# Moving two steps of layer 1 in ScalarE's hand-written order of a graph-attention kernel

## The chip, the cores and the metric

The kernel runs on one core of a Trainium2 chip. The metric is the device time of one execution in microseconds (us); less is better. The kernel before was timed three times: 405.50, 405.58 and 405.77 us, so its median is 405.58 us.

Of the core's engines, TensorE (PE) does the matrix products and writes to PSUM, VectorE (DVE) and GpSimd (POOL) do elementwise work and reductions, ScalarE (ACT) does activations, copies and scalings, and SyncE (SP) only starts transfers here. Each engine works off its own list of instructions in order and waits at semaphores for the others.

## The reference

Sixteen graphs of 512 nodes with 128 features each pass through four layers; every layer adds its input and normalizes each node:

```python
x = _layernorm(x + _L0_gnn_ref(x, adj, ...))   # attention, softmax over a row
x = _layernorm(x + _L1_gnn_ref(x, adj, ...))   # attention, softmax over a column, ELU
x = _layernorm(x + _L2_gnn_ref(x, adj, ...))   # attention, softmax over a row, ELU
x = _layernorm(x + _L3_gnn_ref(x, ...))        # sums over relations, no softmax
```

The change lies in layer 1:

```python
h = x @ W;  s1 = h @ a1;  s2 = h @ a2
e = leaky_relu(s1[:, :, None] + s2[:, None, :], 0.2)
att = softmax(where(adj > 0, e, -9e15), axis=1)     # over the column
h_prime = att @ h
return elu(h_prime)
```

A column without any edge gets equal weights in this softmax (all its entries are -9e15). The kernel calls it an empty column and fills it.

## The kernel before, in words

**Items and slots.** One graph in one layer is an item; items are numbered n = layer * 16 + graph, so layer 1 is items 16 to 31. Each engine runs the function `attention_slot(at, n)` for slot after slot; `at(k)` is item n + k. So in slot n an engine does the late steps of items n-3 to n and the early steps of items n+1 to n+4, in an order that is written out by hand and that is its own for each engine. A slot of layer 1 takes about 7.2 us.

**The way of a layer-1 item k.**
- Slot k-4 and k-3: PE transposes x (L482), ACT copies it (`take_xT`, L720), PE multiplies by the weights (L503), ACT copies the result to `hx` (`take_h`, L725). DVE takes the maximum of a score per partition (`own_max`, L1008), PE spreads it, DVE reduces it to `smax` (`take_max`, L1013).
- Slot k-2: from the scores and `smax`, ACT makes `col_tmp[ABOVE]` by a Relu (`above_max`, L756) and from it `col_tmp[HINGE]` by an Exp (`column_hinge`, L761, the hinge). POOL adds the mark of the empty columns to it and gets `col_tmp[WEIGHT]` (`column_weight`, L313). POOL also makes `col_tmp[BELOW]` (`below_max`, L306).
- Slot k-1: PE spreads BELOW over `rows_ps` (`spread_rows`, L551). ACT makes two exponentials of it, one in `q_rows` (L770) and one in place (L771); together they are `take_rows`. POOL masks the first quarter of the edges (`mask_rows`, L298). DVE makes the other three quarters in `edges` (L1024, three instructions; each needs WEIGHT and the rows) and then the four blocks of the matrix `PT` in `weights` (L1041 for block 0, L1047 for blocks 1 to 3), with the sums of the columns beside them. From these come the reciprocals `col_tmp[RZ]` (`column_sums` L1069, `column_factors` L1073). ACT adds the mark of empty columns to block 0 of `PT` (`fill_empty`, L777; the other blocks get it from DVE by a maximum).
- Slot k: POOL scales h by RZ (`scale_h`, L281), and PE multiplies (`attend`, L566), once `PT` is whole, filled and h scaled.
- Slot k+1: ACT begins the ELU (`elu`, L789 Relu, L799 Exp), POOL adds to it (`elu_low`, L337), DVE finishes the sum (`add_elu`, L1122), takes the moments (`finish` L1128, `aggregate` L1135).
- Slot k+2: POOL makes the reciprocal deviation (`find_rstd`, L319 and L322), ACT scales to the new x (`take_scaled`, L806, four instructions).

**Order on POOL** in a slot of layer 1: `below_max(n+2)`, `mask_rows(n+1)`, `elu_low(n-1)`, `find_rstd(n-2)`, `column_weight(n+2)`, `scale_h(n+1)`. After `scale_h` comes the next slot's `below_max`. **Order on DVE:** `own_max(n+3)`, the four blocks of `PT` of item n+1, `take_max(n+3)`, `column_sums`, `column_factors`, `add_elu(n-1)`, and from slot 17 on the three edge instructions of item n+2 among the moments of item n-1; in slots 15 to 17 the edges of item n+1 stand at the head of the slot. **Order on PE:** transposes, `spread_rows(n+1)`, `project(n+3)`, `attend(n)`. **Order on ACT** before, for layer 1: `take_rows(n+1)`, `elu(n-1)`, `take_h(n+3)`, `take_xT(n+4)`, `above_max(n+2)`, `take_scaled(n-2)`, `fill_empty(n+1)`, `column_hinge(n+2)`.

At the start of layer 1 ACT's slot 15 ends with `flag(15)` (L839, a 2 us pass over the mask), and at the end slots 30 and 31 have `node_factors` of layer 2 (L735 to L751) in them.

Of the kernel before, what the change touches and what calls it, by code (L numbers as in the profile page):

```python
# [54 lines left out]
def build(nc, x, adj, adj_rows, w_in, w_out, a_in, b2, ab2, w3, b3, out):  # L55
    ctx = ExitStack()
    with ctx:
# [8 lines left out]
        def sem(name):  # L66
            if name not in sems:
                sems[name] = ctx.enter_context(nc.semaphore(name))
            return sems[name]
# [628 lines left out]
        def _(act):  # L698
# [34 lines left out]
            def node_factors(it):  # L733
                act.wait_ge(sem("smax"), it.done)
                act.activation(shifts[:, it.b, :], shift_k[:, 0:3], ACT.Copy, scale=smax[:, it.b:it.b + 1])\  # L735
                    .then_inc(sem("shifts"), 1)
                act.wait_ge(sem("shifts"), halves(it))
                if it.l > 0 or it.g >= 2:

                    act.wait_ge(sem("PT"), (it.done - 2) * C)  # L740
                    act.wait_ge(sem("h_scaled"), it.done - 2)
                raw = factors_raw[:, it.b, :, :]
                act.activation(raw[:, 0, :], hx[:, it.r, :, S1], ACT.Relu, scale=1 - SLOPE,
                               bias=shifts[:, it.b, 0:1])
                act.activation(raw[:, 1, :], hx[:, it.r, :, S2], ACT.Exp, scale=1 - SLOPE,
                               bias=shifts[:, it.b, 1:2])
                act.activation(raw[:, 2, :], hx[:, it.r, :, S2], ACT.Exp, scale=SLOPE,
                               bias=shifts[:, it.b, 2:3]).then_inc(sem("factors_raw"), 1)
                act.wait_ge(sem("factors_raw"), halves(it))
                act.activation(factors[:, it.b, 0, :], raw[:, 0, :], ACT.Exp, scale=-1.0)  # L750
                act.activation(factors[:, it.b, 1:3, :], raw[:, 1:3, :], ACT.Identity, bias=floor_col[:, 0:1])\  # L751
                    .then_inc(sem("factors"), 1)

            def above_max(it):
                act.wait_ge(sem("smax"), it.done)
                act.activation(col_tmp[:, it.b, ABOVE, :], hx[:, it.r, :, S2], ACT.Relu, bias=smax[:, it.b:it.b + 1])\  # L756
                    .then_inc(sem("above"), 1)

            def column_hinge(it):
                act.wait_ge(sem("above"), it.of_layer)  # L760
                act.activation(col_tmp[:, it.b, HINGE, :], col_tmp[:, it.b, ABOVE, :], ACT.Exp, scale=SLOPE - 1)\  # L761
                    .then_inc(sem("hinge"), 1)

            def take_rows(it):
                act.wait_ge(sem("rows_ps"), it.done)
                if it.g >= 1:

                    act.wait_ge(sem("edge_lin"), (it.of_layer - 1) * EDGES)
                    act.wait_ge(sem("mask_rows"), (it.of_layer - 1) * WHOLE)
                act.activation(q_rows[:, :], rows_ps[:], ACT.Exp, scale=SLOPE).then_inc(sem("q_rows"), 1)  # L770
                act.activation(rows_ps[:], rows_ps[:], ACT.Exp, scale=1 - SLOPE).then_inc(sem("rows_taken"), 1)  # L771

            def fill_empty(it):

                act.wait_ge(sem("PT"), (it.done - 1) * C + WHOLE)
                for c in range(WHOLE):
                    last = act.activation(PT[:, it.b, c, :], PT[:, it.b, c, :], ACT.Identity,  # L777
                                          bias=empty_col[:, it.g, c:c + 1])
                last.then_inc(sem("filled"), 1)

            def elu(it):

                if it.l > 1 or it.g >= 1:
                    act.wait_ge(sem("elu_exp"), it.done - (G + 1))

                if it.l == 1:
                    act.wait_ge(sem("att"), it.done)
                    lin_ps = o_ps[it.b][:, :, 1:1 + D]
                    act.activation(elu_low_arg[:, :, :], lin_ps, ACT.Relu, scale=-1.0)\  # L789
                        .then_inc(sem("elu_low_arg"), 1)  # L790
                else:
                    act.wait_ge(sem("y_lin"), it.of_layer)
                    act.activation(elu_low_arg[:, :, :], lin[:, it.b, :, :], ACT.Relu, scale=-1.0)\
                        .then_inc(sem("elu_low_arg"), 1)

                if it.done > G + 1:
                    act.wait_ge(sem("y_sum"), it.done - 1)
                act.wait_ge(sem("elu_low_arg"), it.done - G)
                act.activation(elu_exp[:, :, :], elu_low_arg[:, :, :], ACT.Exp, scale=-1.0)\  # L799
                    .then_inc(sem("elu_exp"), 1)  # L800

            def take_scaled(it):

                act.wait_ge(sem("rstd"), it.done)
                for c in range(C):
                    last = act.activation(X[:, it.g, c, :], y[:, it.t, c, :], ACT.Copy, scale=rstd[:, it.t, c:c + 1])  # L806
                last.then_inc(sem("x_new"), 1)

            def take_norm(it):
                act.wait_ge(sem("offset"), it.of_layer)  # L810
                for c in range(C):
                    last = act.activation(X[:, it.g, c, :], y[:, it.t, c, :], ACT.Identity,  # L812
                                          bias=offset[:, it.t, c:c + 1], scale=rstd[:, it.t, c:c + 1])
                last.then_inc(sem("x_new"), 1)
# [28 lines left out]
            def take_bias2(n):  # L843

                for k, part in enumerate((bias2_hi, bias2_mid, bias2_low)):
                    if n == BIAS_SLOT + 5 + k:
                        act.wait_ge(sem("bias2"), 5)
                        row = slice(32 * k, 32 * k + 1)
                        act.copy(bias2_parts[row, 0:130], part[row, :])
                        act.copy(bias2_parts[row, 130:260], part[row, :])  # L850
                        act.activation(bias2_parts[row, 260:260 + D], part[row, 0:D], ACT.Copy, scale=float(N))\
                            .then_inc(sem("bias2_parts"), 1)

            def take_next(at):
                if at(3):
                    take_h(at(3))
                if at(4):
                    take_xT(at(4))
                if at(4) and at(4).done == 1:
                    take_folded_weights()  # L860

            def attention_slot(at, n):
                if at(1) and at(1).l == 1:
                    take_rows(at(1))
                if at(-1) and at(-1).l == 1:
                    elu(at(-1))
                if at(2) and at(2).l in (0, 2):
                    node_factors(at(2))
                if at(-1) and at(-1).l == 2:
                    elu(at(-1))  # L870
                past_first_layer = any(at(k) and at(k).l >= 1 for k in (1, -2))
                if past_first_layer:
                    take_next(at)
                take_bias2(n)
                if at(2) and at(2).l == 1:
                    above_max(at(2))
                if at(-3) and at(-3).l == 0:
                    take_scaled(at(-3))
                if at(-3) and at(-3).l == 2:
                    take_norm(at(-3))  # L880
                if at(-2) and at(-2).l == 1:
                    take_scaled(at(-2))
                if at(1) and at(1).l == 1:
                    fill_empty(at(1))
                if not past_first_layer:
                    take_next(at)
                take_centred(n)
                if at(2) and at(2).l == 1:
                    column_hinge(at(2))
                if n == -1:  # L890
                    act.wait_ge(sem("b2_ps"), 1)
                    act.copy(b2_a[:, :], o_ps[1][:, 0, 0:2]).then_inc(sem("b2_a"), 1)
                if at(0) and at(0).l == 0:
                    flag(at(0))
# [85 lines left out]
            def redo_norm(g, k):  # L980
# [5 lines left out]
                last.then_inc(sem("re_x"), 1)  # L986

            pipeline(attention_slot, FIRST, LAST_ATTENTION, G * LAYERS)
            pipeline(last_layers(attention_slot, relation_slot), LAST_ATTENTION, ALL_STEPS, G * (LAYERS + 1))
            act.wait_ge(sem("out"), 16 * G)  # L990
            with act.If(not_binary(act)):
# [399 lines left out]
```

## Time and profile before

| | |
|---|---|
| median of three runs | 405.58 us |
| the profiled execution | 405.65 us |
| its span, first to last instruction | 403.5 us |
| busy: DVE, PE, ACT, POOL | 87%, 88%, 77%, 76% of the span |
| layer 1 in the span | about 112 to 230 us |
| ACT's steps `take_rows`, `fill_empty`, hinge | 0.99, 0.61 and 0.10 us, start to next start |

The profile shows one execution. Each instruction has a start in us from the beginning of the span, a duration, an engine, a line of the kernel, and, in brackets, how long its engine had been idle before it and which instruction of which engine ended that. Durations of neighbours on one engine overlap a little, so that the distance from start to start is the better price of an instruction in a row. "L313" is line 313 of the kernel. The busy shares are means over all layers; what a step is worth is read from its own stage.

### The profile page before, as it was taken

The page shows a single profiled execution, that of the slowest core. Times are in us where ns is not written, and L with a number is a line of the kernel's source. Part 1 is how long each engine was busy: PE and PEld are TensorE (multiplying, and loading weights), DVE is VectorE, ACT ScalarE, POOL GpSimd, SP SyncE. Part 2 cuts the span into 40 slices and gives each one's busy share as a digit, 9 for nine tenths or more (in the row PEclk, how much of TensorE's full clock was granted, in tenths as well). Part 3 has the DMA queues.
Part 4 walks back from the last instruction along what each step waited for, and adds up shares of the span by engine and source line. Part 5 has one row for each costly group of instructions (what it writes and reads, how often), then busy time and mean ns, then how long its engine had stood idle before and what let it go on. Part 6 is the DMA issues. An engine that isn't in the chain of part 4 may idle for free. (4 is left out here: it accounts for less than half of the span.)

```text
span 403.5 us, 9212 instructions
## 1 busy us (share of the span) xinstructions
PE 354.2 (88%) x2784; PEld 315.7 (78%) x2791; DVE 350.3 (87%) x1350; ACT 310.3 (77%) x845; POOL 306.8 (76%) x399
## 2 busy tenths in 40 slices
PE   7798999999977878788788889999999879799990
PEld 7697999999977778778687889999998776466660
DVE  0558899999999989999999988999999997799975
ACT  2757999999886676776877867688988846888851
POOL 5356888787779778687675776888888885899992
PEclk9999999999999999999999999999999989999997
DMA  6999983000000000000000000000000000012223
GB/s 172 202 246 246 249 167 54 2 1 2 2 1 2 1 2 0 2 2 0 1 2 2 3 0 2 0 3 2 0 4 2 0 2 0 0 72 86 80 79 109
DMA packets 8755, 18.19 MB, mean 45 GB/s; under 512 B 1280, under 2 KB 2560, under 8 KB 8704
## 3 DMA queue, kind: packets, MB, share of 16 engines
q0 software_dynamic: 2304, 8.39, 10.9%
q1 hardware_dynamic: 5280, 8.72, 6.2%
q10 hardware_dynamic: 1120, 0.46, 0.5%
q8 instruction: 24, 0.39, 0.4%
q14 instruction: 27, 0.22, 0.2%
HBM read 21.76 MB, written 4.19 MB: 64 GB/s over the span
## 5 line engine op out<-in xcount | busy, mean ns | idle before, releaser
L566 PE MATMUL o_ps<-h_scaled,PT 128*128 128x129 f32 (+1 forms) x1536 | 182.3, 277 | 9.9 <-POOL h_scaled L281 7.3
L566 PEld LDWEIGHTS o_ps<-h_scaled,PT 128*128 128x128 f32 x1536 | 176.7, 193 | 12.7 <-issue 10.6
L1052 DVE SCALAR_TENSOR_TENSOR PT<-rows_ps,factors,MT 128x512 f32<-128x512 f32 x128 | 89.2, 739 | 0.0
L806 ACT ACTIVATE X<-y,rstd 128x128 f32<-128x128 f32 x184 | 58.4, 389 | 24.7 <-POOL rstd L322 24.7
L322 POOL TENSOR_TENSOR rstd<-var_eps,neg_half 128x4 f32<-128x4 f32 x64 | 70.1, 1095 | 5.0
L503 PE MATMUL h_ps<-wx,xT 128*128 128x130 f32 x384 | 53.5, 283 | 13.8 <-DVE smax L1013 12.2
L503 PEld LDWEIGHTS h_ps<-wx,xT 128*128 128x128 f32 x384 | 48.3, 193 | 19.6 <-issue 19.3
L1128 DVE BATCH_NORM_STATS2 stats<-y 128x6 f32<-128x128 f32 x256 | 55.6, 280 | 5.8 <-DVE y L1122 0.9
L257 POOL TENSOR_TENSOR mean_term<-h_mean,empty_row 128x512 f32<-128x512 f32 x32 | 38.2, 1194 | 9.9 <-DVE residual L1108 5.2
L337 POOL TENSOR_TENSOR elu_exp<-elu_exp,X 128x512 f32<-128x512 f32 x32 | 40.8, 1276 | 5.1 <-ACT elu_exp L799 4.8
L281 POOL TENSOR_TENSOR h_scaled<-hx,factors 128x516 f32<-128x516 f32 x32 | 33.6, 1052 | 12.7 <-PE o_ps L566 8.2
L1024 DVE SCALAR_TENSOR_TENSOR edge<-rows_ps,col_tmp,q_rows 128x512 f32<-128x512 f32 x48 | 34.8, 736 | 4.0 <-ACT rows_ps L771 3.7
L725 ACT COPY hx<-h_ps 128x520 f32<-128x520 f32 x48 | 27.7, 577 | 10.5 <-PE h_ps L507 10.1
L1047 DVE SCALAR_TENSOR_TENSOR PT<-MT,empty_col,edge 128x512 f32<-128x512 bf16 x48 | 34.6, 765 | 0.0
L319 POOL TENSOR_TENSOR var_eps<-mean_var,eps_tile 128x4 f32<-128x4 f32 x64 | 18.3, 286 | 18.8 <-DVE mean_var L1135 18.6
L839 ACT ACTIVATE square_out<-MT,minus_half 128x2048 bf16<-128x2048 bf16 x16 | 32.0, 1998 | 0.0
L482 PE MATMUL xT_ps<-ident,X 128*128 128x128 f32 x192 | 30.0, 280 | 0.9 <-ACT xT L720 0.9
L720 ACT ACTIVATE xT<-xT_ps 128x512 f32<-128x512 f32 x48 | 28.6, 596 | 0.0
L812 ACT ACTIVATE X<-y,offset,rstd 128x128 f32<-128x128 f32 x64 | 26.2, 488 | 1.4 <-POOL offset L331 1.4
L1135 DVE BATCH_NORM_AGGREGATE mean_var<-stats 128x2 f32<-128x6 f32 x256 | 23.9, 156 | 2.3
L1008 DVE TENSOR_REDUCE smax_own<-hx 128x1 f32<-128x4 f32 x48 | 7.0, 147 | 20.6 <-ACT hx L725 20.6
L482 PEld LDWEIGHTS xT_ps<-ident,X 128*128 128x128 f32 x192 | 23.0, 145 | 1.7 <-ACT xT L720 1.6
(123 smaller groups left out, 660.6 us busy)
## 6 DMA issues: line engine op xcount, KB each, us to landing
MT<-adj_by_j POOLq DMA_DIRECT2D x16, 512.0 KB, 14.8
X<-x SPq DMA_DIRECT2D x16, 256.0 KB, 8.1
out<-X SPq DMA_DIRECT2D x16, 256.0 KB, 2.0
w_rel<-w SPq DMA_DIRECT2D x1, 256.0 KB, 6.0
w_back<-w_by_output ACTq DMA_DIRECT2D x1, 192.0 KB, 3.5
wx<-w_by_input ACTq DMA_DIRECT2D x1, 192.0 KB, 4.0
bias<-b ACTq DMA_DIRECT2D x1, 64.0 KB, 3.0
bias_in<-b SPq DMA_DIRECT2D x1, 64.0 KB, 8.3
```

The costliest lines, as they stand in the source:

```text
L257: pool.tensor_tensor(mean_term[:, it.b, :, :], h_mean[:, it.m, :].unsqueeze(1).broadcast_to([P, C, D]), empty_row[:, it.g, :].unsqueeze(2) ...
L281: pool.tensor_tensor(h_scaled[:, it.b, :, first:1 + D], hx[:, it.r, :, first:1 + D], by.unsqueeze(2).broadcast_to([P, C, 1 + D - first]), ...
L322: pool.tensor_tensor(rstd[:, it.t, :], var_eps[:, it.t, :], neg_half[:], ALU.pow)\
L337: pool.tensor_tensor(elu_exp[:, :, :], elu_exp[:, :, :], X[:, it.g, :, :], ALU.add)\
L482: last = pe.transpose(xT_ps[:, c * P:(c + 1) * P], rows[:, c, :], ident[:])
L503: last = pe.matmul(h_chunk_ps(c, 130), xT[:, b, c * P:(c + 1) * P], wx[:, l, :], start=(l != 2), stop=(l != 2 or c == 1))
L566: last = pe.matmul(o_ps[it.b][:, ic, first:1 + D], PT[:, it.b, jc, ic * P:(ic + 1) * P], h_scaled[:, it.b, jc, first:1 + D], start=(jc == ...
L806: last = act.activation(X[:, it.g, c, :], y[:, it.t, c, :], ACT.Copy, scale=rstd[:, it.t, c:c + 1])
L1024: dve.scalar_tensor_tensor(out=edge[:, c, :], in0=rows_ps[:], scalar=col_tmp[:, it.b, WEIGHT, c:c + 1], in1=q_rows[:, :], op0=ALU.max, op1 ...
L1047: dve.scalar_tensor_tensor(out=PT[:, it.b, c, :], in0=m, scalar=empty_col[:, it.g, c:c + 1], in1=edge[:, c, :], op0=ALU.max, op1=ALU.min, ...
L1052: dve.scalar_tensor_tensor(out=PT[:, it.b, c, :], in0=rows_ps[:], scalar=factors[:, it.b, 1, c:c + 1], in1=m, op0=ALU.max, op1=ALU.mult, * ...
L1128: last = dve.bn_stats(stats[:, c, :], y[:, b, c, :])
```

## The change

On ScalarE, in the slots of layer 1, two steps are moved. `column_hinge(n+2)` goes from the end of the slot to just behind `above_max(n+2)`, from whose result it is made. `fill_empty` goes from behind `take_scaled` to the second place of the next slot, behind `take_rows` and ahead of `elu`; since the slot number has gone up by one, it is called with `at(0)` there instead of `at(1)`. ACT's order in a slot becomes `take_rows(n+1)`, `fill_empty(n)`, `elu(n-1)`, `take_h`, `take_xT`, `above_max(n+2)`, `column_hinge(n+2)`, `take_scaled(n-2)`. No instruction is added or removed, and no other engine's list changes.

```diff
@@ def attention_slot(at, n):   # ScalarE
                 if at(1) and at(1).l == 1:
                     take_rows(at(1))
+                if at(0) and at(0).l == 1:
+                    fill_empty(at(0))
                 if at(-1) and at(-1).l == 1:
                     elu(at(-1))
...
                 if at(2) and at(2).l == 1:
                     above_max(at(2))
+                    column_hinge(at(2))
...
                 if at(-2) and at(-2).l == 1:
                     take_scaled(at(-2))
-                if at(1) and at(1).l == 1:
-                    fill_empty(at(1))
                 if not past_first_layer:
                     take_next(at)
                 take_centred(n)
-                if at(2) and at(2).l == 1:
-                    column_hinge(at(2))
```

## Rows read from the trace of the kernel before

**Rows 1.** Who waited for whom, 142 to 223 us (total us, times, longest us)
```profile
POOL col_tmp L313 <- ACT col_tmp L761: 22.9, 12, 2.1
ACT X L806 <- POOL rstd L322: 18.1, 11, 2.0
...
DVE edge L1024 <- ACT rows_ps L771: 3.5, 10, 0.9
```
**Rows 2.** Timeline of POOL, 199.9 to 207.3 us (start us, duration us, instruction, idle before)
```profile
199.94 0.20 POOL L313 TENSOR_TENSOR col_tmp<-col_tmp,big_col 128x4 f32<-128x4 f32 x1 [2.10 <-ACT col_tmp L761]
200.09 1.04 POOL L281 TENSOR_TENSOR h_scaled<-hx,col_tmp 128x512 f32<-128x512 f32 x1
...
202.51 1.28 POOL L337 TENSOR_TENSOR elu_exp<-elu_exp,X 128x512 f32<-128x512 f32 x1
...
204.02 1.03 POOL L322 TENSOR_TENSOR rstd<-var_eps,neg_half 128x4 f32<-128x4 f32 x1
207.15 0.20 POOL L313 TENSOR_TENSOR col_tmp<-col_tmp,big_col 128x4 f32<-128x4 f32 x1 [2.10 <-ACT col_tmp L761]
```
**Rows 3.** Timeline of ACT, 203.8 to 209.3 us
```profile
203.79 0.30 ACT L756 ACTIVATE col_tmp<-hx,smax 128x4 f32<-128x4 f32 x1
205.09 1.28 ACT L806 ACTIVATE X<-y,rstd 128x128 f32<-128x128 f32 x4 [0.99 <-POOL rstd L322]
206.27 0.71 ACT L777 ACTIVATE PT<-PT,empty_col 128x512 f32<-128x512 f32 x1
206.88 0.19 ACT L761 ACTIVATE col_tmp<-col_tmp 128x4 f32<-128x4 f32 x1
206.98 0.57 ACT L770 ACTIVATE q_rows<-rows_ps 128x512 f32<-128x512 f32 x1
...
207.97 0.58 ACT L789 ACTIVATE elu_low_arg<-o_ps 128x512 f32<-128x512 f32 x1
208.64 0.63 ACT L799 ACTIVATE elu_exp<-elu_low_arg 128x512 f32<-128x512 f32 x1
```
**Rows 4.** Timeline of DVE: a passage without wait, then a steady slot
```profile
134.30 0.68 DVE L1122 SCALAR_TENSOR_TENSOR y<-o_ps,elu_exp 128x512 f32<-128x512 f32 x1
135.06 0.75 DVE L1024 SCALAR_TENSOR_TENSOR edge<-rows_ps,col_tmp,q_rows 128x512 f32<-128x512 f32 x1
...
200.86 0.75 DVE L1024 SCALAR_TENSOR_TENSOR edge<-rows_ps,col_tmp,q_rows 128x512 f32<-128x512 f32 x1 [0.27 <-ACT rows_ps L771]
...
204.61 0.74 DVE L1047 SCALAR_TENSOR_TENSOR PT<-MT,empty_col,edge 128x512 f32<-128x512 bf16 x1
...
207.02 0.18 DVE L1073 RECIPROCAL col_tmp<-col_tmp 128x4 f32<-128x4 f32 x1
207.11 0.68 DVE L1122 SCALAR_TENSOR_TENSOR y<-o_ps,elu_exp 128x512 f32<-128x512 f32 x1
```
**Rows 5.** Timeline of PE, 201.4 to 206.2 us
```profile
201.39 3.81 PE L566 MATMUL o_ps<-h_scaled,PT 128*128 128x128 f32 x32 [0.41 <-POOL h_scaled L281]
...
205.58 0.60 PE L551 MATMUL rows_ps<-ident,col_tmp 128*128 128x128 f32 x4
```
**Rows 6.** Timelines of POOL and DVE where small POOL work meets L1047
```profile
133.35 1.42 POOL L322 TENSOR_TENSOR rstd<-var_eps,neg_half 128x4 f32<-128x4 f32 x1
...
154.25 0.39 POOL L345 TENSOR_TENSOR bias<-b_a,ab_sb 128x2 f32<-128x2 f32 x1
...
154.52 0.74 DVE L1047 SCALAR_TENSOR_TENSOR PT<-MT,empty_col,edge 128x512 f32<-128x512 bf16 x1
...
168.69 0.62 POOL L351 TENSOR_TENSOR bias_rest<-bias,bias_hi 128x130 f32<-128x130 f32 x1
...
168.94 0.91 DVE L1047 SCALAR_TENSOR_TENSOR PT<-MT,empty_col,edge 128x512 f32<-128x512 bf16 x1
```
**Rows 7.** Timelines of ACT and DVE near the end of layer 1
```profile
224.94 0.57 ACT L725 COPY hx<-h_ps 128x520 f32<-128x520 f32 x1
...
225.54 0.16 DVE L1008 TENSOR_REDUCE smax_own<-hx 128x1 f32<-128x4 f32 x1
```

## The prediction

> **What bounds the kernel now.** I read the table of waits for the steady part of layer 1 first, then the timelines of POOL, ACT and DVE over one of its slots, then PE's, and last the two ends of the layer. The reader is to see a ring of two engines. In the waits [rows 1], POOL's `column_weight` waits 22.9 us for ACT's hinge, and ACT's `take_scaled` waits 18.1 us for POOL's rstd: each of the two idles for the other, which is the mark of a closed ring. DVE waits only 3.5 us in ten slots, always for `take_rows`. So DVE is nearly full, and the ring is what keeps it from being quite full.
>
> The ring can be added up from one slot. POOL goes from `column_weight` at 199.94 through `scale_h`, `below_max`, `mask_rows`, `elu_low`, `var_eps` to rstd, which starts at 204.02 and takes 1.03, without a gap: 5.11 us [rows 2]. ACT takes over at 205.09 (0.04 later) with `take_scaled`, 1.18 us from start to the next start; then the fill, 0.61; then the hinge, 0.19 [rows 3]; and POOL's next `column_weight` starts at 207.15, 0.08 behind the hinge's end [rows 2]. 5.11 + 0.04 + 1.18 + 0.61 + 0.19 + 0.08 = 7.21 us, which is the distance of the two `column_weight` rows. The hinge needs neither `take_scaled` nor the fill: its input, `above_max`, was done at 204.09, while ACT then idled 0.99 us [rows 3]. It merely stands behind them in ACT's list.
>
> DVE's own list is shorter. From the first edge instruction at 200.86 to the end of `add_elu` at 207.79 it runs for 6.93 us [rows 4]. Where nothing is waited for, the next edge instruction starts 0.08 behind the end of `add_elu` (134.98 to 135.06) [rows 4]. So DVE alone would take 7.01 us a slot, 0.20 less than the ring.
>
> **The change part by part.** Nothing is added or removed, so the sum is about order only.
>
> *The hinge moved up.* It will stand behind `above_max` and wait for its result. The nearest row for such a step is the ELU's Exp, which starts 0.09 behind the end of the Relu it needs (208.55 to 208.64) [rows 3]. So the hinge runs about 0.3 us after the start of `above_max`, at the place of today's 204.2, done at 204.4, all of it inside ACT's idle time before rstd (0.98 to 1.9 us in these slots) [rows 1, 3]. Cost nothing; if that cover were gone it would cost 0.3 us of ACT. `column_weight` then has its input before POOL gets to it, and POOL does it right behind rstd. The ring is opened. What is late next for `scale_h` is its other input, RZ from DVE: done at 207.20, where POOL now starts `scale_h` near 207.30 (207.15 plus the 0.15 from row to row) [rows 2, 4]. With 0.08 for the semaphore, it would start at 207.28: POOL's chain is from now on hung on DVE.
>
> *The fill moved back.* `take_rows` comes 0.61 + 0.10 us earlier behind `take_scaled`, at today's 206.27 instead of 206.98 [rows 3]. It also needs `rows_ps` from PE, whose four transposes end at 206.18 [rows 5], 0.09 before. Then follow the two exponentials, 0.99, the fill, 0.61, and the ELU at its old place: 206.27 + 0.99 + 0.61 = 207.87 against 207.97. So the ELU isn't delayed against rstd, though the fill stands in front of it. The fill ends at 206.27 + 0.99 + 0.71 = 207.97; PE's `attend` also needs h_scaled, which ends 1.04 after 207.28, at 208.32. The fill has 0.35 us in hand and costs nothing. Queued behind `take_rows`'s wait are now the fill and with it `attend`: PE gives `rows_ps` in its list before `attend`, so there is no circle.
>
> *What this does to a steady slot.* I lay out a slot with the first edge instruction at 0 and 7.01 us of DVE. RZ is done at 6.34; `scale_h` starts at 6.42, which is 0.59 before the next edge (before, 200.09 to 200.86: 0.77 before it) [rows 2, 4]. Rstd ends 4.96 later, at 4.37 of the next slot; `take_scaled` starts at 4.41; `take_rows` runs from 5.59 to 6.6 and a bit (0.48 plus 0.58). DVE wants it at 7.01: 0.35 us in hand. Other rings: from rstd over `take_scaled` 1.18, `take_rows` 0.99, the fill 0.61, the ELU 0.67 + 0.63, 0.08, and `elu_low` to the end of rstd, 202.51 to 205.05, 2.54, plus 0.04: 6.74 us. PE from `attend` to the end of `spread_rows`, 201.39 to 206.18, 4.79 [rows 5], then `take_rows` and fill 1.70 and 0.3 to the next `attend`: 6.8 us. All below 7.01, so DVE alone sets the pace.
>
> *The sum.* The ten waits of DVE come to 3.5 us [rows 1]; each leaves the 0.08 that is there anyway: 3.5 - 0.8 = 2.7 us. Two more slots of the twelve show no wait; I count them at nothing. The largest piece is the first, the 0.9 us [rows 1], where ACT has two `take_scaled` in a slot. The slots before it, 15 to 17, gain nothing: DVE is not kept waiting there.
>
> *The end of the layer.* In the fill's last place nothing changes: in slot 31 there is no `take_rows`, so the fill of item 31 has the same neighbours. But ACT's later part of a slot now lies later against DVE: the ELU starts 0.17 after the next edge instruction (4.41 + 1.18 + 0.99 + 0.61 = 7.19, less 7.01, about 0.18), where before it started 0.10 before it (207.97, edge at 208.07). That is 0.28 later. In most slots `hx` has room for it, but in slot 30, with layer 2's factors in ACT's list, `hx` is done at 225.51 and DVE's `own_max` takes it at 225.54 [rows 7]. DVE waits there some 0.25 us, and POOL's chain behind RZ hands it on to layer 2. Bounds for this piece: 0 (if ACT's lag is smaller) and 0.3. I take 0.25. 2.7 - 0.25 = 2.45 us. Behind layer 1 all engines hang on DVE and POOL, and no transfer is due, so I carry the gain to the end unchanged; an estimate, with 0.3 either way.
>
> *A new neighbour.* `column_weight` will run right behind rstd, 4.37 us after the edge, and DVE's first L1047 starts at 3.75 (204.61 less 200.86) and takes 0.74 [rows 4], so that the second starts at about 4.4. Before, it ran when DVE was past its L1047s. The nearest rows are a 128x2 operation of POOL in that very place, 154.25, with 0.39 instead of 0.20, and the L1047 beside it, unhurt at 0.74; and a larger one, 128x130 with two inputs, at 168.69, beside which L1047 took 0.91, 0.17 more [rows 6]. `column_weight` is 128x4, nearest to the first: I take 0 and keep 0.17 a slot. POOL has 2 us to spare there. Such an overlap is the case of a rule of the Trainium skill (SBUF — State Buffer, Who interferes with whom): a VectorE instruction with two SBUF inputs and a GpSimd instruction that reads SBUF exclude each other, and the one that starts first blocks the other. By that rule `column_weight` would wait for the first L1047 and might hold up the second; the row at 154.25 agrees for the first half of it and not for the second. If it held in full, with the 0.20 of `column_weight` lost at L1047 in each of twelve slots, the sum would be 2.4 us worse, 405.6.
>
> 405.65 - 2.45 = 403.2 us. The profiled execution, 405.65, is 0.07 above the median of the runs, 405.58, so I leave it at 403.2.
>
> **The rivals.**
> - *DVE is hurt by the new neighbour.* Each of the twelve steady slots loses 0.17 us at L1047: 2.0 of the 2.45 us are given back, 405.2 us. For it: the row of 0.91 [rows 6]. Against: it stands beside an operation of thirty times the size.
> - *Nothing gained.* The wait for `take_rows` would stay because `rows_ps` is late: PE's rows are only 0.09 us ahead of the new need [rows 3, 5]. If `spread_rows` came 0.55 later than I lay out, the 0.35 in hand and the 0.20 of gain would be gone: 405.6. Against: `spread_rows` hangs on `scale_h` by a fixed 4.79 + 0.26 us, which I have counted.
> - *Slower: POOL slides into DVE's L1047.* POOL's chain lies 0.18 us later against DVE. Rstd took 1.42 instead of 1.03 where it began inside an L1047 (133.35) [rows 6]. If var_eps and rstd both slid in and took 0.4 more each, the ring over fill and ELU would be 6.74 + 0.8 = 7.54 us, 0.33 above today's slot, 12 x 0.33 = 4.0: 409.6 us. The point from which it decides: the chain would have to start 0.7 us later against DVE (rstd begins at 3.34 and var_eps 0.3 ahead of it, the first L1047 at 3.75 [rows 4]). Against: a steady shift of 0.18 is what the sum gives. The same rule of the Trainium skill bears on it, and the 1.42 agrees with it.
> - *More than I say.* No loss at the layer's end, the two uncounted slots give their few hundredths, and layer 2 starts better: 402.6.
>
> **How the numbers follow.** Forecast 0.62 (402.9 to 403.7); more gain 0.09; neighbour 0.12; nothing 0.11; slower 0.06. A change within 0.2% (0.8 us) is about what a measurement of this kernel can't tell from none. Of the neighbour's share a third lies past 0.8 us, since it need not cost the full 0.17. Faster 0.75, same 0.18, slower 0.07. The range from 402.4 to 405.2 takes in the forecast, more gain and the neighbour, and leaves out nothing and slower, 0.17.
>
> **What would show it.** Right: POOL's L313 loses its 22.9 us of waits for L761, and L281 waits for DVE's L1073 instead, up to 2 us a slot; L1024's waits for L771 vanish; slots of 7.0 us; ACT still waits for rstd about 1.5 us. At the end of the layer L1008 waits 0.2 to 0.3 for L725. Wrong: L1047 of 0.9 beside L313; L319 of 0.6 or L322 of 1.4 in the steady slots; PE waiting for the fill; slots that stay at 7.2.

## The result, and the profile after

The changed kernel takes 401.75 us (median of 8 runs, 400.24 to 403.54); the kernel before took 405.50 us beside it (8 runs, 404.32 to 405.77). The ratio is 0.9903, with a 95% interval of 0.9885 to 0.9921: faster by 3.75 us. The forecast was 403.2 us in a range of 402.4 to 405.2, so the sign and the mechanism were right and the size was not: the gain was half as large again as forecast. The profiled execution took 401.82 us with a span of 399.7 us, against 405.65 and 403.5 before: 3.83 us by the one and 3.8 by the other.

First the waits of the steady part of layer 1 in the changed kernel, 139 to 221 us, as in [rows 1] (engine, line, waited for whom: total us, times, longest us; VectorE's line numbers are one lower than before, those of POOL, PE and of the ACT rows shown here are the same):

```profile
ACT X L806 <- POOL rstd L322: 13.3, 12, 1.5
POOL h_scaled L281 <- DVE col_tmp L1072: 11.5, 12, 1.8
...
PE o_ps L566 <- ACT PT L777: 0.5, 1, 0.5
DVE edge L1023 <- ACT rows_ps L771: 0.2, 1, 0.2
```

POOL's 22.9 us of waits for the hinge [rows 1] are gone, and POOL waits for VectorE's reciprocals instead. VectorE's 3.5 us have shrunk to 0.2. The ring of POOL and ACT is open; VectorE now sets the pace. PE's wait of 0.5 us for the fill comes once, at 142.91, near the start of the stretch, and so does VectorE's 0.2.

The timeline of VectorE in a steady slot, which answers to [rows 4], shows how full it is (start, duration, instruction):

```profile
183.05 0.68 DVE L1121 SCALAR_TENSOR_TENSOR y<-o_ps,elu_exp 128x512 f32<-128x512 f32 x1
183.65 0.74 DVE L1023 SCALAR_TENSOR_TENSOR edge<-rows_ps,col_tmp,q_rows 128x512 f32<-128x512 f32 x1
...
189.80 0.18 DVE L1072 RECIPROCAL col_tmp<-col_tmp 128x4 f32<-128x4 f32 x1
189.89 0.68 DVE L1121 SCALAR_TENSOR_TENSOR y<-o_ps,elu_exp 128x512 f32<-128x512 f32 x1
190.49 0.74 DVE L1023 SCALAR_TENSOR_TENSOR edge<-rows_ps,col_tmp,q_rows 128x512 f32<-128x512 f32 x1
```

From edge to edge are 6.84 us, not the 7.01 of the forecast. The edge instruction starts 0.60 us after `add_elu` started, which is 0.08 before the record of `add_elu` ends. The forecast had it 0.08 behind that end.

The chain that feeds VectorE, on ACT and POOL, as in [rows 2, 3]:

```profile
187.14 1.03 POOL L322 TENSOR_TENSOR rstd<-var_eps,neg_half 128x4 f32<-128x4 f32 x1
188.14 0.73 POOL L313 TENSOR_TENSOR col_tmp<-col_tmp,big_col 128x4 f32<-128x4 f32 x1
190.05 1.04 POOL L281 TENSOR_TENSOR h_scaled<-hx,col_tmp 128x512 f32<-128x512 f32 x1 [1.19 <-DVE col_tmp L1072]
```
```profile
188.20 1.28 ACT L806 ACTIVATE X<-y,rstd 128x128 f32<-128x128 f32 x4 [0.93 <-POOL rstd L322]
189.39 0.57 ACT L770 ACTIVATE q_rows<-rows_ps 128x512 f32<-128x512 f32 x1
189.86 0.58 ACT L771 ACTIVATE rows_ps<-rows_ps 128x512 f32<-128x512 f32 x1
```

`take_rows` ends at 190.44, and VectorE's edge instruction starts at 190.49. So the chain has no time in hand at all any more: it and VectorE's own list arrive together. And at the end of the layer, as in [rows 7] (VectorE, then ACT):

```profile
221.50 0.16 DVE L1007 TENSOR_REDUCE smax_own<-hx 128x1 f32<-128x4 f32 x1 [0.53 <-ACT hx L725]
```
```profile
220.90 0.57 ACT L725 COPY hx<-h_ps 128x520 f32<-128x520 f32 x1
```

### The profile page after: what moved, and what is told of

Its sections match the earlier page's. It is cut to its first block and busy times, and to the rows that moved or that the text cites. A ratio compares the mean times of both kernels' runs of the same rounds, so it can differ in the third digit from the quotient of the medians.

```text
span 399.7 us, 9212 instructions
## 1 busy us (share of the span) xinstructions
PE 354.1 (89%) x2784; PEld 315.8 (79%) x2791; DVE 349.2 (87%) x1350; ACT 311.5 (78%) x845; POOL 313.5 (78%) x399
## 5 line engine op out<-in xcount | busy, mean ns | idle before, releaser
L503 PEld LDWEIGHTS h_ps<-wx,xT 128*128 128x128 f32 x384 | 48.3, 193 | 17.1 <-issue 16.9
L1046 DVE SCALAR_TENSOR_TENSOR PT<-MT,empty_col,edge 128x512 f32<-128x512 bf16 x48 | 34.5, 763 | 0.0
L281 POOL TENSOR_TENSOR h_scaled<-hx,col_tmp 128x512 f32<-128x512 f32 x16 | 16.7, 1042 | 14.2 <-DVE col_tmp L1072 14.2
```

The source lines that it names most:

```text
L281: pool.tensor_tensor(h_scaled[:, it.b, :, first:1 + D], hx[:, it.r, :, first:1 + D], by.unsqueeze(2).broadcast_to([P, C, 1 + D - first]), ...
L503: last = pe.matmul(h_chunk_ps(c, 130), xT[:, b, c * P:(c + 1) * P], wx[:, l, :], start=(l != 2), stop=(l != 2 or c == 1))
L1046: dve.scalar_tensor_tensor(out=PT[:, it.b, c, :], in0=m, scalar=empty_col[:, it.g, c:c + 1], in1=edge[:, c, :], op0=ALU.max, op1=ALU.min, ...
```

## The experiments

The quickest measure is the distance from one reciprocal `col_tmp[RZ]` of VectorE to the next, one per slot: it can be read to 0.01 us in one profiled execution, while the times of a kernel scatter by 3 us (400.24 to 403.54 in the changed one; on that below). The distances are called slots here. In the changed kernel they are, after a first one of 7.10, 6.84 to 6.86 us, and 7.01 to 7.02 in two slots beside POOL's bias work; in the kernel before 7.21, with 7.05 to 7.50 beside that work.

The theory I went in with (A in the expectations): VectorE's own list takes 6.84 us a slot. Just under it lies a ring over two slots: from the edge instruction to the reciprocal 6.33, then `scale_h`, `below_max`, `mask_rows`, `elu_low`, rstd, `take_scaled`, `take_rows` and the next edge 7.35, together 13.68, or 6.84 a slot. The rival (B): the hinge, for which POOL waited 22.9 us, was all that mattered.

The cuts of edits below are against the changed kernel, and the comments in them are the document's.

**e1 and e10: the hinge alone.** The fill stays behind `take_scaled`.

```diff
-                if at(0) and at(0).l == 1:
-                    fill_empty(at(0))
...
                     take_scaled(at(-2))
+                if at(1) and at(1).l == 1:
+                    fill_empty(at(1))
```

> Only the hinge moves up; the fill stays behind take_scaled. Theory A (a second, two-slot ring over POOL's chain, take_scaled and take_rows lies just under VectorE's own pace): the one-slot ring is open, but the fill's 0.61 us still stands between take_scaled and take_rows, so the two-slot ring is 13.68 + 0.61 = 14.29 us, 7.15 a slot. VectorE waits for take_rows still, about 0.3 a slot. Against the kernel before 0.06 a slot in twelve slots, about 0.8 us: 404.8 (before 405.6). Theory B (the hinge alone was the chain, as the waits of POOL for it suggest): all of the gain, slots of 6.85, 401.8.

> e1 once more with more rounds, since its times (403.5 to 406.8) scatter more than what is to be seen. In the layer's steady slots 7.46 and 6.85 in turn, as in e1. Theory: by the slots 0.8 to 1.0 us below the kernel before wherever TensorE's clock behaves alike; a drop of the granted clock near 129 us costs 1.0 us when it comes. 404.7 without it, 405.7 with it. Rival: the hinge alone is worth nothing or less.

Measured: 406.13 us (4 runs), ratio 1.000 [0.9964, 1.0036]; again 405.89 us (12 runs) against 405.88, ratio 0.9999 [0.9984, 1.0014]. The last six steady slots of e1 are 7.46, 6.84, 7.46, 6.85 and so on, 7.15 on the mean, as forecast. The alternation is the mark of a ring that closes once in two slots. VectorE in e1:

```profile
200.27 0.74 DVE L1023 SCALAR_TENSOR_TENSOR edge<-rows_ps,col_tmp,q_rows 128x512 f32<-128x512 f32 x1
...
207.72 0.75 DVE L1023 SCALAR_TENSOR_TENSOR edge<-rows_ps,col_tmp,q_rows 128x512 f32<-128x512 f32 x1 [0.52 <-ACT rows_ps L771]
...
214.57 0.75 DVE L1023 SCALAR_TENSOR_TENSOR edge<-rows_ps,col_tmp,q_rows 128x512 f32<-128x512 f32 x1
```

In one slot VectorE waits for `take_rows`, in the next it doesn't. POOL doesn't wait for the hinge any more (its waits are 16.9 us for VectorE's reciprocals instead). So B falls: removing a wait of 22.9 us in full, at its cause, brought nothing that the times can show. The 0.8 us that I expected in the time aren't there either; the interval ends at 0.65. Both profiled executions had the drop of the clock described below, which eats as much as the slots gain. The stretch of the trace from POOL's first rstd to its last, which leaves out the scatter at both ends (see e4), is 363.32 us before and 363.22 and 363.02 in e1 and e10, drop included. Whether the drop comes more often with this kernel, or whether the gain is lost otherwise, stays open.

**e2 and e11: the fill alone.** The hinge stays at the end of the slot.

```diff
                     above_max(at(2))
-                    column_hinge(at(2))
...
                 take_centred(n)
+                if at(2) and at(2).l == 1:
+                    column_hinge(at(2))
```

> Only the fill moves back; the hinge stays behind take_scaled. Theory A: the one-slot ring is 7.21 - 0.61 = 6.60 us, under VectorE's pace, so the hinge where it is costs only its 0.10 between take_scaled and take_rows: the two-slot ring is 13.78, 6.89 a slot. Nearly all of the gain: 402.3. POOL still waits for the hinge in the profile, and it means nothing. Theory B: POOL's wait for the hinge stays, and so does most of the time: 404.5 or more.

> e2 once more with more rounds. Steady slots 6.94 and 6.86 in turn. Theory: 402.2 without the drop of the clock near 129 us, 403.2 with it; so 0.5 us above the changed kernel beside it. Rival (the hinge's place matters by more than its 0.10 us): 404.4 again, 2.7 above.

Measured: 404.37 us (4 runs), ratio 0.9966 [0.9939, 0.9993]; again, with more runs, 402.87 us (6 runs), ratio 0.9926 [0.9905, 0.9948], beside 402.24 for the changed kernel. Its steady slots are 6.94 and 6.86 in turn, 6.90 on the mean; 6.89 was expected. From first rstd to last e11's profile takes 359.92 us, 3.4 less than the kernel before, where the changed one has 4.05 less. And POOL still waits for the hinge in e2 (142 to 221 us):

```profile
POOL col_tmp L313 <- ACT col_tmp L761: 15.3, 12, 1.5
```

Two thirds of POOL's 22.9 us are still there, as the longest wait of the table, and four fifths of the gain have been had, by e11's times and by its trace (3.0 of 3.6 us, 3.4 of 4.05). It is the fill's place that mattered, in two rings at once: in the one-slot ring with the hinge, and in the two-slot ring between `take_scaled` and `take_rows`. By e2's own four runs (404.4) it would be a third of the gain only; the two intervals overlap, and e2's profiled execution had the drop of the clock. The share rests on the slots and on e11.

**e4 and e12: the changed kernel again**, on the same chips as e1 to e3 and e9 to e11.

> The changed kernel once more, beside the others on the same chip: 401.8 us, slots of 6.85.

> The changed kernel beside these three: 401.7 by the median, slots of 6.85; 400.8 where no clock drop comes near 129 us by the slots before it, 1 us more where one comes.

Measured: 401.64 us (4 runs, 400.84 to 404.27), ratio 0.9913 [0.9875, 0.9951], and 402.24 us (6 runs), ratio 0.9916 [0.9895, 0.9937]. The steady slots are 6.84 to 6.87 in both, beside the bias work 7.01 to 7.02. The profiled execution of e4, at 404.27 us, shows where some of the scatter comes from. TensorE, then VectorE, then three stretches of e4: their length, the busy times of PE, its weight loads, VectorE, ACT and POOL with the number of instructions, and behind the last bracket the mean granted clock (1.00, 0.74, 0.69) and the DMA share and GB/s:

```profile
129.74 5.31 PE L566 MATMUL o_ps<-h_scaled,PT 128*128 128x128 f32 x32 [0.82 <-POOL h_scaled L281]
```
```profile
135.63 0.29 DVE L1012 TENSOR_REDUCE smax<-h_ps 128x1 f32<-128x128 f32 x1 [0.89 <-PE h_ps L531]
```
```profile
124.00:128.00 4.00, 2.55 (x24) 2.33 (x23) 3.96 (x16) 1.62 (x4) 3.54 (x4) 1.00 0.00 0
128.00:131.00 3.00, 2.18 (x14) 2.02 (x14) 3.00 (x9) 2.94 (x9) 2.90 (x6) 0.74 0.04 8
131.00:134.00 3.00, 3.00 (x21) 3.00 (x21) 3.00 (x16) 0.81 (x3) 1.76 (x3) 0.69 0.00 0
```

One `attend` took 5.31 instead of 3.81 us, since the granted clock was 0.50 from 129.5 to 132.5, that is 1.2 instead of 2.4 GHz. TensorE had idled 1.45 us up to 127.79 and 0.82 up to 129.74, with 1.13 us of work between. VectorE had to wait 0.89 us, and this slot took 8.28 instead of 7.30. The drop is there, near 129 us, in the profiles of e1, e2, e4, e5, e7 and e10, and in that of e9 one `attend` earlier, at 120 us (5.44 us). It is not in layer 1 in those of the kernel before, the changed one, e3, e6, e11 and e12, with the same idle times at that place (1.44 to 1.46 and 0.82 to 0.83 us).

Most other drops cost nothing that the trace shows. In nine of the fourteen profiles the clock is at 0.5 for some time between 318 and 333 us, behind layer 1. In six of these (the kernel before, the changed one, e2, e3, e11 and e12) it lasts 3 to 4 us, and POOL's rstd rows beyond it keep their distances to 0.1 us; in e5 it lasts 6.6 us, and they come 0.7 later. The rest of the scatter lies at the two ends: the first rstd starts between 33.60 (e3) and 35.37 us (e4), and behind the last one come between 5.7 and 6.9 us more. Between the two rstds the changed kernel takes 359.27 and 359.12 us in the two profiles without the drop in layer 1, and 360.18 in e4, so the drop is worth 1.0 us.

**e5, e6, e7: what bounds the steady slot.** In layer 1, e5 leaves out the first of the four instructions of `take_scaled`, e6 the first of the four `bn_stats` of VectorE, e7 both.

```diff
-                for c in range(C):                            # take_scaled
+                for c in range(1 if it.l == 1 else 0, C):
...
-                for c in range(C):                            # moments
+                for c in range(first, C):                     # first = 1 in layer 1
```

> The changed kernel, with the first of take_scaled's four instructions left out in layer 1 (so block 0 of x isn't renewed there). The rings over take_scaled get about 0.3 us shorter, VectorE's list stays. Theory A (VectorE alone sets 6.84 a slot): nothing moves, 401.8. Rival (VectorE is full only because everything hangs on the two-slot ring): 0.15 a slot less, slots of 6.7, 400.1.

> The changed kernel, with the first of the four bn_stats of VectorE left out in layer 1 (the statistics of block 0 are stale there). VectorE's list gets 0.20 us shorter (0.22 at most), to 6.64. The two-slot ring holds that piece once in two slots: 13.68 - 0.20 = 13.48, 6.74 a slot. Theory A: the slot falls to 6.74 and VectorE waits for take_rows 0.1 to 0.2 again; 1.1 us less than the changed kernel, 400.7. Rival (VectorE alone, no ring near): 6.64, 2.3 us less, 399.5.

> Both cuts, take_scaled and bn_stats, each one of four instructions in layer 1. VectorE 6.64, two-slot ring (13.68 - 0.20 - 0.30) / 2 = 6.59. Theory A: 6.64, 2.3 us less than the changed kernel: 399.5. If e5 and e6 each give little and this one much, two bounds lie side by side.

Measured, two runs each: e5 402.1 us, ratio 0.9883 [0.981, 0.9957], slots 6.84 to 6.87; e6 400.7 us, ratio 0.9849 [0.9782, 0.9917], the last slots 6.74 to 6.75; e7 400.4 us, ratio 0.9842 [0.977, 0.9914], slots 6.65 and 6.82 in turn, 6.735 on the mean. No changed kernel ran beside them, so the slots decide and not the times. e5 and e6 came as theory A has them, e5's slots unmoved, e6's half of the way that VectorE's list got shorter. So VectorE is the bound at 6.84, and the two-slot ring stands right behind it. e7 didn't: 6.64 was expected, since both bounds I knew of were cut. TensorE, ACT and VectorE of e7 in one of its long slots:

```profile
202.71 0.60 PE L551 MATMUL rows_ps<-ident,col_tmp 128*128 128x128 f32 x4
```
```profile
202.21 0.99 ACT L806 ACTIVATE X<-y,rstd 128x128 f32<-128x128 f32 x3 [0.49 <-POOL rstd L322]
203.34 0.60 ACT L770 ACTIVATE q_rows<-rows_ps 128x512 f32<-128x512 f32 x1
203.84 0.59 ACT L771 ACTIVATE rows_ps<-rows_ps 128x512 f32<-128x512 f32 x1
```
```profile
204.46 0.75 DVE L1023 SCALAR_TENSOR_TENSOR edge<-rows_ps,col_tmp,q_rows 128x512 f32<-128x512 f32 x1
```

ACT is through with `take_scaled` at 203.20, but takes the rows only at 203.34, 0.03 behind PE's last transpose, 203.31. The third bound is the rows' way over PE: reciprocal to the next edge 7.32 us by that way (197.14 to 204.46), and 6.14 back, 13.46 in two slots, 6.73 a slot. The prediction had seen PE's rows "0.09 before" ACT's need; I had left it out of the expectation of e7. With VectorE's 0.20 us put back this ring is 13.66, 6.83 a slot. So in the changed kernel three bounds lie within 0.02 us of each other, and e6's 13.48 can't tell the two rings apart.

**e8: the fill one place later still**, behind the ELU.

```diff
-                if at(0) and at(0).l == 1:
-                    fill_empty(at(0))
                 if at(-1) and at(-1).l == 1:
                     elu(at(-1))
+                if at(0) and at(0).l == 1:
+                    fill_empty(at(0))
```

> The changed kernel with the fill one place later, behind the ELU instead of ahead of it. The fill ends 1.3 us later, 0.9 us behind the start of PE's attend as it is. Then PE, take_rows, ELU and fill are one ring in one slot: 4.83 + 0.99 + 0.67 + 0.54 + 0.71 + 0.25 = 8.0 us. Theory: slots of 8.0, some 14 of them, 15 us more than the changed kernel: 417. Rival (PE has idle time to hide it): 402 to 403.

Measured: 423.3 us (2 runs), ratio 1.0405 [1.0332, 1.0478]. Five of the slots are 7.86 us, near the 8.0 expected, and six are 9.49, so that the time is 6 us above the 417 expected. TensorE in e8, and two of its stretches (granted clock behind the last bracket):

```profile
180.19 3.81 PE L566 MATMUL o_ps<-h_scaled,PT 128*128 128x128 f32 x32 [1.90 <-ACT PT L777]
...
188.05 5.44 PE L566 MATMUL o_ps<-h_scaled,PT 128*128 128x128 f32 x32 [1.90 <-ACT PT L777]
```
```profile
188.00:190.00 2.00, 1.95 (x12) 1.98 (x13) 2.00 (x10) 1.32 (x4) 1.92 (x3) 0.70 0.04 8
190.00:192.00 2.00, 2.00 (x12) 2.00 (x11) 2.00 (x5) 1.28 (x4) 1.53 (x3) 0.50 0.00 0
```

PE waits 1.90 us for the fill in ten slots and 1.4 in three more, so the ring PE, `take_rows`, ELU, fill is real and has nearly the size worked out for it. What I hadn't expected is the second price: in six of the ten the clock falls to half behind that idle time, and the slot takes 1.63 us more, 10 us in all. So the place "ahead of the ELU" is worth some 20 us, about half of them by the clock: the fill has some 0.3 us in hand there, and an ELU's length too late it holds up everything.

**e3 and e9: a version that beats both.** e3 takes the 0.53 us at the end of the layer away: in slot 30 alone, ACT copies `hx` and its neighbours ahead of layer 2's first factors. e9 has that too, and POOL makes `column_weight` ahead of `find_rstd` in slots 15 to 17. (The line that sets `past_first_layer` moves up with the first edit.)

```diff
+                next_first = at(1) and at(1).l == 1 and at(2) and at(2).l == 2
+                if next_first:
+                    take_next(at)
                 if at(2) and at(2).l in (0, 2):
                     node_factors(at(2))
...
-                if past_first_layer:
+                if past_first_layer and not next_first:
                     take_next(at)
```
```diff
+                weight_ahead = n <= G + 1                      # e9 only, POOL
+                if weight_ahead and at(2) and at(2).l == 1:
+                    column_weight(at(2))
                 if at(-2):
                     find_rstd(at(-2))
...
-                if at(2) and at(2).l == 1:
+                if not weight_ahead and at(2) and at(2).l == 1:
                     column_weight(at(2))
```

> The changed kernel, and in slot 30 alone ScalarE copies hx, h_mean and xT of the next items ahead of layer 2's first factors. Theory: VectorE's wait of 0.53 us for hx at the end of layer 1 is a loss that is carried to the end; it goes: 0.5 us less than the changed kernel, about 401.3. Rival: the factors, now 1.3 us later, hold up PE's spread_rows of item 32 and the loss comes back: 401.8 or more.

> e3's kernel, and in slots 15 to 17 alone POOL makes column_weight ahead of find_rstd instead of behind it. Theory: the edge instruction at 135.06 us in the kernel before, and at 135.09 in the changed one, did wait, for column_weight's 134.97, though no wait is marked; with the weight ready earlier it starts 0.60 us behind the start of add_elu instead of 0.77. 0.17 us less there and 0.5 at the layer's end: about 401.0 where the changed kernel has 401.7. Rival (0.08 us between add_elu and the edge is VectorE's own): the distance stays at 0.76 to 0.77.

Measured: e3 401.52 us (4 runs), ratio 0.9896 [0.9869, 0.9923], beside the changed kernel's 0.9913 [0.9875, 0.9951]: the times can't tell them apart (401.3 was expected). The trace can: `own_max` in slot 30 starts behind the edges without a wait, and the last distance is 6.84 instead of 7.48, 0.64 us less. The rival falls: PE's `spread_rows` of item 32 didn't wait for the factors. e9 took 400.88 us (4 runs, 400.57 to 401.33), ratio 0.9872 [0.9854, 0.9889], the lowest of all; the changed kernel beside it 0.9916 [0.9895, 0.9937]. VectorE and POOL of e9 where [rows 4] had its "passage without wait":

```profile
134.15 0.68 DVE L1127 SCALAR_TENSOR_TENSOR y<-o_ps,elu_exp 128x512 f32<-128x512 f32 x1
134.75 0.74 DVE L1029 SCALAR_TENSOR_TENSOR edge<-rows_ps,col_tmp,q_rows 128x512 f32<-128x512 f32 x1
```
```profile
130.82 0.20 POOL L313 TENSOR_TENSOR col_tmp<-col_tmp,big_col 128x4 f32<-128x4 f32 x1
...
138.54 1.59 POOL L322 TENSOR_TENSOR rstd<-var_eps,neg_half 128x4 f32<-128x4 f32 x1
```
```profile
138.49 0.74 DVE L1052 SCALAR_TENSOR_TENSOR PT<-MT,empty_col,edge 128x512 f32<-128x512 bf16 x1
```

With the weight done at 131.02 instead of 134.97, the edge instruction starts 0.60 us behind the start of `add_elu`; it was 0.77 in the changed kernel (134.32 to 135.09) and 0.76 in the kernel before. So that row had been a wait for `column_weight`, which the profile doesn't mark. In the next slot POOL's rstd started 0.05 us inside an L1052 (which is L1047 of the kernel before) and took 1.59 instead of 1.03, and that slot took 7.69 instead of 7.10. In the changed kernel the same two lie 0.02 us apart (138.84, 138.86) and rstd takes its 1.03, so it was a matter of hundredths; whether the edit or the drop of the clock at 120 us shifted them isn't shown. That drop lengthened the slot of 7.30 to 7.61. With both losses the trace of layer 1 as a whole is no shorter than the changed kernel's (first reciprocal to last 106.10 us against 105.93), though two pieces of 0.19 and 0.63 us are gone from it. The times are 1.3 us lower, and the intervals don't overlap; 0.7 was expected (401.0 against 401.7). What the other half is stays open.

## Why the prediction was wrong in size and right in kind

**The one-slot ring: right.** Its 7.21 us were added up from rows, and when the change opened it POOL's waits for the hinge vanished and `scale_h` hung on L1072 instead, as forecast.

**VectorE's own pace: the step that failed.** The term of the sum that was mis-sized is the gain in the twelve steady slots, 2.7 us, and it was so by one reading. "Where nothing is waited for, the next edge instruction starts 0.08 behind the end of `add_elu`" rested on 134.98 to 135.06 [rows 4]. That was a wait after all, for `column_weight`, as e9 showed. Without one, the next instruction starts before the record of the one ahead ends, 0.60 us after its start. VectorE's slot is 6.84 to 6.85 us instead of 7.01, and the difference of 0.16 came in eleven of the twelve slots: 1.8 us. (In the first the rows still come late, 142.20, and the distance is 0.84.) The same rows had the right number all along: every other pair of neighbours in VectorE's timeline overlaps by such an amount. With it the sum becomes 2.7 + 1.8 = 4.5 us. Row by row, the distance from `add_elu` to the edge instruction shrinks by 4.52 in the twelve slots, 0.39 of it in the two that the prediction counted at nothing. The trace has 4.65 over all: from the edge instruction of item 19 to that of item 31 are 87.44 us before (135.06 to 222.50) and 82.79 after (135.09 to 217.88).

**The end of the layer: right place, half the size.** I took 0.25 us with bounds of 0 and 0.3; it was 0.53. The lag of ACT behind VectorE was worked out with slots of 7.01; with 6.84 the ELU starts later still against the edge (218.37 against 217.88 in slot 30, 0.49 us, where I had 0.18). Both errors are one error: with 6.84 for 7.01 in the prediction's layout, rstd ends 0.17 later in the slot, the slot ends 0.17 earlier, and 0.18 becomes 0.52. By the distances of the reciprocals the loss is 0.58, 7.48 less 6.84 after against 7.27 less 7.21 before. 4.65 - 0.58 = 4.07, and POOL's rstd rows behind layer 1 lie 4.05 to 4.08 us earlier than before, all through layers 2 and 3: the gain is carried to the end as forecast. The span is 3.8 shorter; the missing 0.3 is behind the last rstd.

**The other rings: right, and nearer than I said.** The two-slot ring was given "0.35 us in hand"; 13.68 us were the right length for it, but with VectorE at 6.84 nothing is left in hand. e1 and e2 show the ring at 14.31 and 13.80, as far as the fill and the hinge lengthen it. The fill itself had "0.35 us in hand": in the steady slot of the changed kernel it is done at 191.08 and PE's `attend` starts at 191.35.

**The new neighbour: right.** `column_weight` now starts inside an L1046 of VectorE (188.06 to 188.80) and takes 0.73 us instead of 0.20 (0.63 to 0.73 in ten of the twelve slots); it ends at 188.87. VectorE's next L1046, from 188.74, takes its 0.75. So POOL is held and VectorE isn't, and POOL had the time: it idles 1.19 us behind it. The Trainium skill (SBUF — State Buffer, Who interferes with whom) has the second of the two fully blocked by the first; the trace agrees for POOL's operation and not for VectorE's. A larger operation of POOL does hold VectorE: the 0.91 of [rows 6] is there again, 181.73, beside bias work that started at 181.14. The forecast slower case, POOL's rstd sliding into an L1047, didn't come in the steady slots, but e9 met it once, with 0.56 us on rstd and 0.59 on the slot, where the prediction had 0.4 for each instruction hit.

## What to carry to other kernels

A long wait in the profile names a ring, not its price. Moving the hinge removed 22.9 us of waits and brought nothing that the times showed; moving the fill left 15.3 us of them and brought most of the gain. Add up each ring, over two slots as well as over one, and compare it with the fullest engine's own list; and price that list by the distances from start to start of rows that are known to wait for nothing, since a small wait isn't marked, and 0.16 us a slot was here 1.8 us.

Where a step is moved to a place with 0.3 us in hand, the next place may cost far more than the move gained: here 1.0 to 2.6 us a slot, for a gain of 0.37.

## What the runs showed of the hardware

- TensorE's granted clock fell from 1.00 to 0.5 (2.4 to 1.2 GHz) for some 3 us behind idle times of 1.45 and 0.82 us near 129 us in six of fourteen profiles and near 120 us in one more, and behind an idle time of 1.90 in six of ten slots of e8. An `attend` that lay in it took up to 5.44 us instead of 3.81 (5.31 in e4), and e4's trace 1.0 us more. A drop of 3 to 4 us between 318 and 333 us moved no rstd row behind it by more than 0.1 in six profiles, one of 6.6 us moved them by 0.7 (e5). Why it comes in one execution and not in another with the same idle times isn't shown.
- A 128x4 operation of POOL took 0.73 instead of 0.20 us when it started 0.08 us inside a VectorE instruction with two SBUF inputs, and rstd 1.59 instead of 1.03 when it started 0.05 us inside one (e9); started 0.02 us inside one, it took its 1.03 (changed kernel, 138.86).
